# First attention: the row maximum reaches the exponential as ScalarE's bias, not by a product on TensorE

## What is computed

```
scores = einsum('bhqd,bhkd->bhqk', q, k) * SCALE
esc    = einsum('bhqd,bhkd->bhqk', eq, ek) * SCALE * decay      # decay[i, j] = exp(-0.1 |i - j|)
attn   = softmax(scores + 0.5 * esc, axis=-1)
ctx    = einsum('bhqk,bhkd->bhqd', attn, mixed)                 # mixed: the values, mixed by gates
out    = ctx @ Wo.T + bo
x      = layernorm(x + (layernorm(hs + out) * ln_g + ln_b))
```

## Time and profile before

| | |
|---|---|
| median of 3 runs | 437.12 us (434.36 to 437.15) |
| the profiled execution | 435.68 us, of which its span 433.9 us |
| PE busy | 369.3 us (85%) |
| DVE busy | 321.4 us (74%) |
| ACT busy | 217.3 us (50%) |
| POOL busy | 154.3 us (36%) |
| L1358 (maxima), 256 instructions and 256 reads | 66.8 and 36.3 us on DVE |
| L616 (the product that subtracts), 64 | 25.0 us on PE, mean 391 ns |
| L1027 (Exp 128x512), 64 | 38.2 us on ACT, mean 597 ns |

### The profile page before, as it was taken

How to read it: one execution, slowest core, us unless ns; L and a number is a source line. 1 busy time by engine, 2 the same in 40 slices (tenths; PEclk the granted TensorE clock), 3 DMA queues, 4 the chain that set the end, 5 groups by cost and what they waited for, 6 DMA issues and landing times.

```text
span 433.9 us, 11945 instructions
## 1 busy us (share of the span) xinstructions
PE 369.3 (85%) x3657; PEld 261.0 (60%) x3666; DVE 321.4 (74%) x1388; ACT 217.3 (50%) x463; POOL 154.3 (36%) x274
## 2 busy tenths in 40 slices
PE   3694879888888888999699999999889979699892
PEld 2573556666566666676467777776557546366461
DVE  6574869999999999997756767677854577564464
ACT  1436657666666665667457667664452411212110
POOL 9657534555555554465543332320110000000000
PEclk9997999999999999999989999999999999999898
DMA  6878866566666665533433333440000000000000
GB/s 136 214 137 160 209 145 113 128 105 118 108 116 113 113 119 105 91 54 85 107 83 99 96 88 109 101 101 3 2 1 2 1 2 24 0 26 1 0 24 25
DMA packets 45161, 35.38 MB, mean 82 GB/s; under 512 B 20736, under 2 KB 41808, under 8 KB 43584
## 3 DMA queue, kind: packets, MB, share of 16 engines
q1 hardware_dynamic: 44080, 34.29, 37.6%
q0 software_dynamic: 512, 0.48, 0.9%
q10 hardware_dynamic: 528, 0.10, 0.1%
HBM read 24.37 MB, written 10.49 MB: 80 GB/s over the span
## 4 chain that ended last, share of the span: by engine, by line
issue 43%; PE 26%; DVE 22%; POOL 4%; ACT 2%; DVEq 1%; DMA 1%; POOLq 0%; ACTq 0%
DVE bank L1358 5%; PE bank L684 5%; PE bank L637 4%; DVE shift L1358 4%; PE bank L666 3%; PE bank L659 3%; PE bank L696 3%; PE bank L807 2%; PE bank L705 2%; DVE res L1429 1%; DVE top L1369 1%; PE bank L616 1%; DVE bv_cols L1288 1%; DVE pf L1257 1%; PE bank L701 1%
## 5 line engine op out<-in xcount | busy, mean ns | idle before, releaser
L1358 DVE CUSTOM_DVE_ANT_0 bank<-bank,decayed_e 128x128 f32<-128x128 f32 x256 | 66.8, 322 | 1.0
L1027 ACT ACTIVATE prob<-bank 128x512 f32<-128x512 f32 x64 | 38.2, 597 | 47.7 <-PE bank L616 46.8
L1369 DVE TENSOR_REDUCE top<-bank 128x4 bf16<-128x512 f32 x64 | 44.2, 690 | 22.0 <-PE bank L637 21.5
L1215 ACT ACTIVATE stk<-bank 128x512 f32<-128x512 f32 x32 | 19.1, 597 | 71.6 <-PE bank L934 71.6
L1627 DVE TENSOR_TENSOR stk<-bank,stk 128x512 f32<-128x512 f32 x32 | 22.1, 692 | 41.0 <-PE bank L941 29.1
L1347 DVE TENSOR_TENSOR decayed_e<-bank,decay 128x512 f32<-128x512 f32 x64 | 43.7, 683 | 6.0 <-issue 5.5
L950 PEld LDWEIGHTS bank<-w,stk 128*128 128x128 f32 x256 | 33.2, 191 | 20.2 <-issue 8.9
L430 POOL TENSOR_TENSOR rest<-pf,parts 128x512 f32<-128x512 f32 (+1 forms) x32 | 29.3, 917 | 42.8 <-ACT parts L1016 42.8
L436 POOL TENSOR_TENSOR parts<-rest,parts 128x512 bf16<-128x512 f32 (+1 forms) x32 | 29.4, 918 | 33.0 <-ACT parts L1020 32.9
L950 PE MATMUL bank<-w,stk 128*128 128x128 f32 x256 | 34.4, 277 | 7.8 <-DVE fres L1638 6.5
L568 POOL TENSOR_TENSOR frstd<-fveps,minus_half 128x4 f32<-128x4 f32 x4 | 4.0, 1010 | 100.9 <-DVE fveps L1648 100.9
(11 more groups left out here) (209 smaller groups left out, 839.6 us busy)
## 6 DMA issues: line engine op xcount, KB each, us to landing
stk<-parts_dram SPq DMA_DIRECT2D x128, 64.0 KB
parts_dram<-parts SPq DMA_DIRECT2D x16, 384.0 KB, 5.3
stk<-parts_dram SPq DMA_DIRECT2D x112, 32.0 KB
stk<-parts_dram SPq DMA_DIRECT2D x16, 192.0 KB
parts_dram<-parts SPq DMA_DIRECT2D x16, 192.0 KB, 2.4
stk<-parts_dram SPq DMA_DIRECT2D x16, 128.0 KB
w<-in_L_ffn_w_dram SPq DMA_DIRECT2D x3, 512.0 KB, 15.4
stk<-parts_dram SPq DMA_DIRECT2D x16, 96.0 KB
```

The lines of the kernel that those rows point to most:

```text
L1027: act.activation(prob[g % 2][:].rearrange("p h t -> p (h t)"), bank[g % 2][:], ACT.Exp).then_inc(L.exped, 1)
L1358: m = dve.tensor_tensor_reduce(out=bank[g % 2][:, 128 * j:128 * j + 128], in0=bank[g % 2][:, 128 * j:128 * j + 128], in1=decayed_e[:, g % ...
L1369: dve.tensor_reduce(top[:, b.par, GH * g:GH * g + GH], bank[0][:].rearrange("p (h t) -> p h t", h=GH), AX.X, ALU.max).then_inc(L2.maxed, 1)
```

## The change

The query side of both projections is made with the opposite sign (scale -SCALE, and the bias with it), so the scores in the bank are the negated ones; DVE keeps the row minimum of them, which is the negated maximum, in an f32 column `neg_max`. The product L616 and its function go. The Exp reads the bank with scale -1 and the column as its bias, and since a bias is one column per instruction, it is now four instructions of 128x128 in place of one of 128x512. ACT waits for the last of the four minima in place of the product; DVE's minima wait for the exponential of u-2 in place of the product of u-2.

```
-            def subtract_max(b, g):
-                u = b.n * NG + g
-                pe.wait_ge(L1.maxed, u + 1)
-                pe.matmul(bank[g % 2][:].rearrange("p (h t) -> p h t", h=GH), neg_ident[:],
-                          shift[:, g % 2, :].unsqueeze(2).broadcast_to([128, GH, S]),
-                          start=False, stop=True, skip_group_check=True).then_inc(L1.shifted, 1)
...
             def exponent(L, b, g):
                 u = b.n * NG + g
-                act.wait_ge(L.shifted, u + 1)
+                act.wait_ge(L.maxed, u + 1)
                 if not isinstance(u, int) or u >= 2:
                     act.wait_ge(L.turned, u - 1)
-                act.activation(prob[g % 2][:].rearrange("p h t -> p (h t)"), bank[g % 2][:], ACT.Exp
-                               ).then_inc(L.exped, 1)
+                for j in range(GH):
+                    e = act.activation(prob[g % 2][:, j, :], bank[g % 2][:, 128 * j:128 * j + 128], ACT.Exp,
+                                       bias=neg_max[:, g % 2, j:j + 1], scale=-1.0)
+                e.then_inc(L.exped, 1)
...
-                    dve.wait_ge(L1.shifted, u - 1)
+                    dve.wait_ge(L1.exped, u - 1)
                 carry(3)
-                with nc.allow_low_precision(reason="the shift cancels"):
-                    for j in range(GH):
-                        m = dve.tensor_tensor_reduce(
-                            out=bank[g % 2][:, 128 * j:128 * j + 128], in0=bank[g % 2][:, 128 * j:128 * j + 128],
-                            in1=decayed_e[:, g % 2, j, :], scale=1.0, scalar=-3.0e38, op0=ALU.add, op1=ALU.max,
-                            accum_out=shift[:, g % 2, j:j + 1])
+                for j in range(GH):
+                    m = dve.tensor_tensor_reduce(
+                        out=bank[g % 2][:, 128 * j:128 * j + 128], in0=bank[g % 2][:, 128 * j:128 * j + 128],
+                        in1=decayed_e[:, g % 2, j, :], scale=1.0, scalar=3.0e38, op0=ALU.add, op1=ALU.min,
+                        accum_out=neg_max[:, g % 2, j:j + 1])
```

More of the change, by code:

```diff
@@ L161, in build @@
         decayed_e = sb("decayed_e", [128, 2, GH, S])
-        shift = sb("shift", [128, 2, GH], BF16)
+        neg_max = sb("neg_max", [128, 2, GH])
         top = sb("top", [128, 2, H], BF16)
@@ L712, in unit1 @@
                     score(b, g)
[L713 to L716, removed]
+                ub, ug = unit_back(b, g, 2)
+                if ub.live:
+                    turn(ub, ug)
                 ub, ug = unit_back(b, g, 3)
@@ L1003, in take_projection @@
                 act.activation(pf[:, 0, 0, :], bank[6][:, 0:128], ACT.Identity, bias=bias_q[:, layer:layer + 1],
-                               scale=SCALE).then_inc(L.proj_ev, 1)
+                               scale=-SCALE if decayed else SCALE).then_inc(L.proj_ev, 1)
                 col = 2 if decayed else 5
@@ L1254, in entangled @@
                 dve.memset(waiter[:, 1:2], 0.0)
-                dve.tensor_scalar(pf[:, 0, 1, :], bank[6][:, 128:256], bias_t[:, 1:2], SCALE * ENT, ALU.add, ALU.mult
+                dve.tensor_scalar(pf[:, 0, 1, :], bank[6][:, 128:256], bias_t[:, 1:2], -SCALE * ENT, ALU.add, ALU.mult
                                   ).then_inc(L1.ent_ev, 1)
@@ L1277, in _ @@
             after(n)
-            step(dve.tensor_scalar(bias_q[:, 0:1], bias_t[:, 0:1], SCALE, None, ALU.mult))
+            step(dve.tensor_scalar(bias_q[:, 0:1], bias_t[:, 0:1], -SCALE, None, ALU.mult))
             n = step(dve.tensor_scalar(bias_q[:, 1:2], bias_t[:, 4:5], SCALE, None, ALU.mult))
```

## The result

| | before | after |
|---|---|---|
| median, same chip | 436.4 us (20 runs, 431.11 to 441.38) | 439.41 us (20 runs, 436.47 to 445.58) |
| ratio, with its 95% interval | | 1.0097 [1.0064, 1.013] |
| the profiled execution, its span | 435.68, 433.9 us | 437.73, 435.9 us |
| PE busy | 369.3 us | 363.6 us |
| DVE busy | 321.4 us | 323.6 us |

What follows compares the result with a forecast made beforehand. It took DVE to bound the first attention's loop. Terms 1.8 - 1.1 - 0.3 + 0.2 gave +0.6 us on the profiled 435.68, so 436.3, stated as 436.6 for the runs' spread; range 425 to 439.5.

Steps and rivals of the forecast that it cites:

- DVE bounds the loop, the product is worth nothing there: First attention's loop: DVE is busy 97.45 of 100 us and PE waits for it, so removing L616 gains 0.
- The way from the minimum to the end of the exponential: Loop: 1.24 us in place of 1.08, 0.16 longer, hidden because the pick needing it comes a unit later.
- L430 at 4.72, L1445 at 4.86, the stall 1.10: Loop slots, from L1003's start: POOL's L430 starts 0.20 later but first, L1445 grows from 0.90; nine slots, +1.8 us.
- The flip: Rival: L430 starts after L1445, freeing DVE in the loop; 424.5 to 426, or 430 in part; chance 0.28.
- L1429 unchanged: Loop: L436's start against L1429 hangs on DVE itself, so L1429's stall behind it stays; 0 us.
- The last slots, -1.1: L1525's 0.49 us wait for L828 goes in three slots as PE gets there earlier; -1.1 us (0 to -1.5).
- PE's clock: Rival: less PE work halves its clock in the loop; 440 and above; 0.10, shared with a supposedly hidden wait.
- The price of a drop: Loop: each stretch of 3 us with PE's clock at half costs some 1.5 us.
- Three decide: Loop: three half-clock stretches of 3 us are enough to bring the time to 440 and above.
- the +0.2 of the start: From 38 to 57 us, short units whose scores do wait for the Exp; +0.2 us (0 to +0.5).
- the -0.3 of the last Exp: Last Exp ends 0.16 later, but PE's transposes no longer queue behind the product (0.39); -0.3 us.
- the forecast's neighbours: Outcomes near the forecast, with POOL still first, 434 to 439 us; chance 0.62 together with the forecast.

Runs made afterwards that it cites:

- a_mid2: Kernel after, with norm_x1 and centre each moved on DVE between the second and third minimum of a unit (g = 3 and g = 0); 424.54 us.
- b_mid2: Kernel before, with norm_x1 and centre both moved on DVE in between the maxima; 429.32 us.
- the swap: Kernel after, with DVE's norm_x1 put ahead of res_stats in unit g = 3; 441.29 us (the same edit in the kernel before: 436.87 us).
- the split: Kernel before, product kept, with the exponential made four instructions of 128 columns, each with a column of zeros as bias; 429.75 us.
- the second profile of after: Profile from measuring the kernel after once more with no edit; 439.37 us, ratio 1.0064.
- the fillers: Kernel after, with one or two products of 512 columns added on PE ahead of each unit's transposes; 438.03 us with one, 437.88 us with two.

## Why the prediction was wrong, point by point

- **DVE bounds the loop, the product is worth nothing there: right.** No time came from it; DVE stayed at 96.64 of 100 us. ACT came to 81.93, not 87, largely as 100 us hold fewer units than before. That freeing DVE makes the product count (a_mid2 against b_mid2) is the other side of it.
- **The way from the minimum to the end of the exponential, 1.24 us, hidden: right.** The step of the exponentials measured 0.26 us (four in 1.14 or 1.15, in 28 of the 40 units from 57 to 165 us) and 0.28 in the unit of each slot that stands ahead of the cast (1.21), and DVE's pick waits, behind the loop's entry, only where the clock is down. The Trainium skill (ScalarE: Activation LUTs, on the cost of an ACTIVATE) gives 0.29 by an estimate; the runs lie nearer the row.
- **L430 at 4.72, L1445 at 4.86, the stall 1.10: right**, measured 4.75, 4.85 and 1.13 to 1.14; eight slots +1.7 us where +1.8 stood for nine.
- **The flip did not come**, though 0.04 us less was left of the margin than forecast (0.10). One thing in its working was wrong: with a margin of 0 DVE would not have been free. In the swap it was ahead by 0.09 and stood. In the split it was ahead by 0.21 and did not. The point from which that rival decides is thus 0.1 to 0.2 us further off than where I put it, and its 0.28 was too much. The Trainium skill (SBUF — State Buffer, who interferes with whom) says that who issues first has the shared pair for the whole instruction; the runs agree with an exclusive hold (1.33 us of stall against 0.33), and add that the start in the record is not the moment that decides.
- **L1429 unchanged: right** (1.22 at 90.61).
- **The last slots, -1.1: failed.** The three waits of 0.49 us ahead of L1525 are gone, as forecast, and a wait of 1.19 stands in their place, behind the stretch from 198.5 to 201.9 in which the clock is down, and PE late from it. The four slots took 1.1 us more (41.16 against 40.10). In the second profile of after they took 40.51, also with a drop in them, and L1518 waited 0.26: part of the gain may be there, but less than a drop costs.
- **PE's clock, given 0.10 with another rival: this is the step that failed.** The sum had no term for it, and three drops in the loop and the last slots cost 2.7 to 3.3 us. The prediction said "72% busy is above the 61% at which the clock held", and named the clock row below 1.00 in the loop as a sign of being wrong; that sign came, 0.97. Its sentence sets a mean over the loop beside one stretch of 3 us. The mean itself was off: 38 products at the row's 0.39 are 15 us, at the step of 0.22 they are 8.4, and 7.8 went (87.47 to 79.63), so it is 80% in after. But a slot's work is uneven: the stretch ahead of each drop has 1.84, 1.85 and 2.00 of 3.40 us busy, 54 to 59%, and was 2.42 before the change. To find it I would have had to lay the change onto the slot at L1429, where DVE stands and PE waits for it, and see that the transposes move ahead of that gap. The third drop, in the last slots, has another gap ahead of it: PE waits 1.32 us there for the exponential. The rows don't tell which gap brings a drop: 122.40:125.80 has 1.79 and is followed by none. In two profiled executions of after two of the loop's slots had one, in that of before none.
- **The price of a drop, "some 1.5 us": too high.** A slot with one lasts 11.82 or 11.68 us against 10.71, 1.0 to 1.1 more (11.91 and 11.95 in the second profile of after), and the next is somewhat shorter, so the two together cost 1.8 and 2.2 us in the two profiles. Over the 75 executions of before that were timed with the experiments, time falls by 2.7 us for each 0.01 of mean clock; a drop of 3.4 us to half is 0.5 x 3.4 / 436 = 0.0039 of it, about 1.06 us. That is a correlation, and it can't be laid on the change as a whole: the medians of the clock lie 0.0145 apart, which would be 3.9 us without the port's part. "Three decide" was right in number: three drops between 60 and 205 us, at 0.9 to 1.1, are 2.7 to 3.3 us.

The sum by what was measured, from the first to the thirteenth L1438: +1.7 for the port, +1.8 for the two drops of the loop, and +1.1 in the last four slots with the third drop: +4.6 us; the second profile of after has +4.3. The change as a whole measured +3.0 by the medians, and +4.2 and +2.8 by the ratios of its two measurements. The ends carry no term. The first long L1438 lies at 77.02 in one profile of after and at 78.53 in the other, and from the thirteenth on the rest lasts 231.75 us in before and 230.42 in after, but 230.6 and 232.0 in two variants of before and 228.9 to 232.2 in those of after. So neither the +0.2 of the start nor the -0.3 of the last Exp can be seen. Less the three drops the same stretch would be +1.3 to +1.9, an estimate within the forecast's neighbours. How the measured 3 to 4 us divide between port and clock is known to about 1 us only, since the fillers, which take the drops away, have a cost of their own; and whether PE's gap at L1451 or its load as a whole brings the drops is argued, not shown.

## What to carry to other kernels

Look at PE's load where it is thinnest in the period of a loop, not at its mean, before taking work off an engine that isn't the bound: the work taken away may be what keeps its clock up, and moved neighbours can make one gap out of two. Where two engines contend for a port, find who is first and by how much, and move the short instruction clear ahead by some tenths of a microsecond: here two moved calls gave 14.9 us, where the change itself had cost 3. A change that is worth nothing while another engine is the bound is worth measuring again once that bound is gone.

## What was not expected of the hardware

- A DVE instruction whose record starts up to 0.10 us ahead of POOL's (0.09 in the swap) still lost the port to it; 0.21 us ahead it kept it. For the other pair, DVE was ahead by 0.03 and lost (100.75 and 100.78 above), and by 0.06 and kept it: the boundary is another for another form of instruction.
- The clock dropped for 3.4 us at a time with no gap of PE longer than 1.37 us in the 3.4 us ahead of it, and in the loop PE then worked through the drop without a pause, 3.40 of 3.40.
- Adding three ACT instructions per unit made the kernel 6.4 us faster, as they delayed a POOL instruction by some tenths of a microsecond.
